# A graph attention layer: the last stage's node tiles in alternating instead of falling order of degree

## The reference

```python
qkv = x @ qkv_w + qkv_b                       # q: 32, k: 32, v: 64 columns
qe = q[s] * scale + (edge_attr @ q_rpe_w + q_rpe_b)
ke = k[t] + (edge_attr @ k_rpe_w + k_rpe_b)
ve = v[t] + (edge_attr @ v_rpe_w + v_rpe_b)
compat = einsum('ehd,ehd->eh', qe, ke)
attn = softmax of compat over the edges of node s
out = segment_sum(ve * attn, s)
return layernorm(x + out)
```

## Time and profile before

| | us |
|---|---|
| median of 3 runs | 5642.24 (5641.77 to 5651.28) |
| profiled execution | 5704.77 |
| its span | 5703.1 |
| busy: TensorE, VectorE | 4020.2, 4190.8 |
| busy: ScalarE, GpSimd | 2869.4, 3574.7 |
| the last stage in the span | about 5107 to 5703 |

### The profile page before, as it was taken

The page is one execution under the profiler, slowest core; times in us unless marked ns, Lnnn a source line. Parts: engine busy times, 40 slices in busy tenths (PEclk is TensorE's granted clock), DMA queues, the critical chain, the costliest instruction groups (busy, mean ns, idle before and its releaser), DMA issues. The chain is left out here.

```text
span 5703.1 us, 94294 instructions
## 1 busy us (share of the span) xinstructions
PE 4020.2 (70%) x18783; PEld 3567.5 (63%) x18783; DVE 4190.8 (73%) x18085; ACT 2869.4 (50%) x6600; POOL 3574.7 (63%) x3772
## 2 busy tenths in 40 slices
PE   7776776676667676776676666767766776649886
PEld 6666666666666666666666666666666666637765
DVE  7777777777777777777777777777777777759997
ACT  3554555555445554554554455545555555424555
POOL 2566666666666666666666666666666666647887
PEclk6555555555555555555555555555555555559998
DMA  6333333333333333333333333333333333379996
GB/s 184 105 109 108 106 108 106 106 110 108 104 104 108 107 105 109 106 109 104 106 112 104 106 106 106 109 106 108 108 106 108 107 107 108 104 175 384 367 351 234
DMA packets 379094, 759.55 MB, mean 133 GB/s; under 512 B 143060, under 2 KB 206875, under 8 KB 365883
## 3 DMA queue, kind: packets, MB, share of 16 engines
q1 hardware_dynamic: 255493, 385.24, 23.0%
q0 software_dynamic: 123520, 373.41, 18.2%
HBM read 570.54 MB, written 187.75 MB: 133 GB/s over the span
## 5 line engine op out<-in xcount | busy, mean ns | idle before, releaser
L634 POOL DMA_INDIRECT rec_dram<-recs,place_i x3223 | 3088.6, 958 | 1872.2 <-issue 1819.0
L670 DVE SCALAR_TENSOR_TENSOR matches<-ids_b,src_f,ps_const 128x128 bf16<-128x128 int16 (+3 forms) x3232 | 1647.3, 543 | 628.4 <-issue 580.4
L786 PE MATMUL ps_feat<-w_in,edge_in 51*128 51x128 f32 x6464 | 1684.2, 438 | 30.5 <-issue 30.4
L769 PE MATMUL ps_look<-free_rec,lo_hotT 128*128 128x98 f32 x6464 | 1609.4, 431 | 2.4 <-ACT lo_hotT L812 2.4
L786 PEld LDWEIGHTS ps_feat<-w_in,edge_in 51*128 51x128 f32 x6464 | 1441.4, 325 | 177.2 <-issue 177.2
L769 PEld LDWEIGHTS ps_look<-free_rec,lo_hotT 128*128 128x128 f32 x6464 | 1473.0, 333 | 2.6 <-ACT lo_hotT L812 2.6
L760 PE MATMUL ps_cnt<-hi_hot,lo_hot 128*128 128x98 bf16 x3232 | 407.2, 277 | 1458.8 <-DVE hi_hot L661 699.6
L824 ACT ACTIVATE free_rec<-ps_cnt 128x98 f32<-128x98 f32 x808 | 194.8, 241 | 2418.2 <-remote 2290.0
L760 PEld LDWEIGHTS ps_cnt<-hi_hot,lo_hot 128*128 128x128 bf16 x3232 | 238.6, 127 | 1671.2 <-issue 818.1
L679 DVE CUSTOM_DVE_ANT_0 picked<-hi_hot,ps_look 128x98 f32<-128x98 bf16 x3232 | 643.9, 249 | 79.1 <-issue 76.4
L812 ACT ACTIVATE lo_hotT<-lo_hotT,one 128x512 f32<-128x512 f32 x808 | 572.9, 709 | 0.0
(11 more groups left out here) (187 smaller groups left out, 2280.6 us busy)
## 6 DMA issues: line engine op xcount, KB each, us to landing
ids_b<-id_dram SPq DMA_DIRECT2D x808, 384.0 KB
rec_dram<-recs,place_i POOLq DMA_INDIRECT x3223
edge_in<-in_attr SPq DMA_DIRECT2D x808, 36.0 KB
w_in<-kv_dram SPq DMA_DIRECT2D x808, 12.0 KB
qx_dram<-qx SPq DMA_DIRECT2D x1, 4753.0 KB, 42.6
kv_dram<-kvt SPq DMA_DIRECT2D x14, 336.0 KB, 3.7
xt<-in_xT SPq DMA_DIRECT2D x14, 224.0 KB, 3.8
origin<-in_dst_tiles SPq DMA_DIRECT2D x1, 1616.0 KB, 7.7
```

The source lines that it names most:

```text
L634: pool.indirect_dma_start(rec_dram[:, :], bass.IndirectOffsetOnAxis(place_i[j][:, m:m + 1], 0), recs[j][:, m, 0:ROW], None).then_inc(scatt ...
L670: last = dve.scalar_tensor_tensor(matches[j % NS][:, junk:junk + before], ids_b[j][:, 1, 0:before], src_f[:, bass.ds(u * CT + m, 1)], ps_c ...
L769: last = nc.tensor.matmul(ps_look[j % NS][:, m, 0:NB], lo_hotT[j % NS][:, P * m:P * (m + 1)], free_rec[j % 2][:, :], start=True, stop=True)
L786: last = nc.tensor.matmul(ps_feat[j % 2][:, m, :], edge_in[j][0:K_ROWS, tile], w_in[j][0:K_ROWS, :], start=True, stop=True)
```

## The change

The order of the tiles' ranks in the last stage. The three of fewest slots stay first. Before, the others followed in falling order of slots. Now the places take in turn the rank with the fewest slots that is left and the rank with the most, from both ends to the middle, and the ranks 92 to 94 (28 slots each) come last.

```diff
 AHEAD = RB + 2
-RANK_OF = [NB - 1, NB - 2, NB - 3, *range(NB - 3)]
+TURNS = NB - 6
+RANK_OF = [NB - 1, NB - 2, NB - 3, *((k - 1) // 2 if k % 2 else TURNS - 1 - k // 2 for k in range(TURNS)), *range(TURNS, NB - 3)]
```

## The result

The changed kernel takes 5668.87 us (median of 6 runs, 5656.94 to 5677.33) where the kernel before takes 5646.76 us (6 runs, 5637.91 to 5656.27) on the same chip. The ratio of the runs is 1.0032, with a 95% interval of 1.0021 to 1.0043, so the change costs 18 us (12 to 24); the two medians lie 22 us apart, which is inside that interval. In the two traces the last stage, from its first record gather to the end of the span, takes 607.9 us after (it starts at 5047.3) and 595.4 us before (from 5107.7): 12.5 us more. What lies ahead of it is not touched by the change and differs between any two executions. The traced execution of the changed kernel is the fastest of its six (5656.94 us).

A forecast was written before the change was run, and what follows sets the result against it. VectorE was taken to bound most of the last stage, GpSimd its end; 0 - 0.7 + 4.0 + 1.3 + 0.4 + 1.5 + 0.3 = 6.8 us on the 5642.24 us median gave 5649 us, range 5637 to 5665.

The forecast's parts named there:

- TensorE's clock: Large tile's sum after a group's square-root stall runs at lowered clock; about five groups hit, +1.5 us, bounds 0 and 4.
- TensorE's window at full clock: TensorE's sum and logits edge behind a large tile outlast VectorE's shorter step; +4.0 us, bounds 0 and 8.
- The cover of the exponentials: VectorE's dot of a small tile is too short to cover ScalarE's exponentials of a large one; +1.3 us, bounds 0 and 3.
- The gathers: Large tiles' gathers have less slack before GpSimd needs them; +0.3 us, bounds 0 and 5.
- The start: Third gather is 29 slots instead of 67, so a 3.38 us wait goes; VectorE then waits 2.7 us; -0.7 us.
- The groups' cover: At a group's square root the covering dot is the small one, less cover early and more late; +0.4 us.
- Slots moved to the end: 73 slots move to the last 14 places: 6.5 us saved under VectorE, 6.6 us lost under GpSimd; together 0.
- No net effect: Rival: small tiles' spare window absorbs delayed large tiles and the start's gain comes in full; about 5642 us, chance 0.20.
- GpSimd's lag: Rival: GpSimd falls behind VectorE until its products delay TensorE's sums, and gathers come late; about 5660 us, chance 0.16.
- One of the signs: Signs of GpSimd falling behind: TensorE's sum waits for GpSimd's products, or the logits' maximum waits for GpSimd's L1238; no size.
- The gathers were not the bound: Rival: DMA engines pace the stage up to 5500 us and alternation evens their load; 5630 us, chance 0.07.

The follow-up runs named there:

- Keeping TensorE busy: Unread matmuls added behind sums ahead of TensorE's gaps; ratio to the kernel before 1.0013 in the changed order (1.0015 with none from place 80), 0.9997 in the old order.
- the pair with half sums: Kernel before and changed kernel, each with every second portion of TensorE's sums left out; ratios to the kernel before 0.9993 and 1.0007.
- Rising: Kernel before with tiles after the first three in rising order of slots, 28-slot tiles last; 5719.69 us, ratio 1.0012.
- heavy end: Kernel before in falling order, but its eleven tiles of 36 and 37 slots moved to places 84 to 94; 5707.75 us, ratio 1.0014.
- the turns with TensorE kept busy: Kernel before with small and large tiles alternating only at places 3 to 83, plus unread matmuls behind sums before place 80; 5701.45 us, ratio 1.0008.

## Why the prediction was off, point by point

The forecast was 5649 us, 6.8 us above 5642.24, with no measurable change as the likeliest outcome (0.63). The kernel became measurably slower, for which the prediction had 0.31. The ratio of 1.0032 on 5642.24 us is 5660 us, inside the range of 5637 to 5665 and above the forecast's own 5643 to 5658. The direction of the sum and its place were right, and so was the mechanism in the main, large sums that miss their window. The size was too small by about half of the stage's 12.5 and 15.9 us. That it came this near is in part luck: one term was far too small and another too large.

- *TensorE's clock.* This is the step that failed most: "about five groups are hit, less where it fitted before: +1.5", with 4 as the upper bound. Keeping TensorE busy gives 7.7, 8.5 and 9.2 us back in places 4 to 45 in three comparisons of traces, and 1.4 us in the order of before. On the chip that ran both orders both ways, 7.7 less 1.4 leaves 6.3 us for the term; the pair with half sums puts it at 6.9 to 9.5. By the medians less comes back, 4.3 and 6.6 us. I had the price of one hit about right but counted only the stalls of groups. The turns make a gap of their own at every pair: TensorE has the small tile's sum done in 3.4 us and then stands for 1.3 and 0.55 us, and behind such gaps, too, the clock fell (5121.50).
- *TensorE's window at full clock.* "Sum 3.4 us" was too much: at undisturbed sums the maximum waited 0.54 us (58 slots; 0.63 predicted) and 0.22 us (54; 0.46 predicted), and the sums of 50 to 45 slots fitted, unless GpSimd's products were late, where I had them 0.1 to 0.3 us short. The 67-slot tile waited 1.86 us and not 3.2. With TensorE kept busy the maximum waits 5.4 us in places 4 to 45 and 0.9 us in the order of before, and at most 3.5 us of that is GpSimd's. So the term is about 1 us where I had 4.0.
- *GpSimd's products.* The forecast had no term for them. They are worth about 3 us: 3.7 and 2.7 us of the waits in the two traces after, nothing before. Together with clock and window the maximum waits 10.0 and 10.4 us more in the two pairs of traces.
- *The cover of the exponentials*, +1.3: held, with 1.8 us measured.
- *The gathers*, +0.3: right in one trace, too small in the other. Behind the dot of place 4 they cost VectorE 0.2 and 2.2 us in places 4 to 45, and nothing before.
- *The start*, -0.7: about right. The dot of place 4 comes 4.1 us sooner, of which 2.8 us is work put off, so -1.3 us. VectorE waits 2.00 us for the 67-slot tile in it (5069.83), where the prediction had 2.7.
- *The groups' cover*, +0.4: VectorE waits 5.6 us for the roots in places 4 to 45 against 4.8 and 4.9.
- *Slots moved to the end*, 0: held. The last stretch left over 13.1 us against 13.2, and its steps are (81.0 - 74.6) / 13 = 0.49 us longer, as the 0.5 predicted.
- *The rivals.* No net effect is out: four traces of alternating orders with whole sums and nothing to keep TensorE busy all leave over 23 to 26 us early. GpSimd's lag gave the nearest number, 5660, and is a part of the cause. One of the signs that the prediction named for it, TensorE's sum waiting for GpSimd's products, is there. The other is not: TensorE did wait for the known part more often (11.4 us in 8 times, 4.3 before), but no wait for the maximum beyond the first followed. Its price was not the 6 us of waits and up to 5 for gathers, but about 3 us and up to 2. The gathers were not the bound either: the DMA share fell as the time rose.

What stays open: the maximum's 10.0 us, the cover's 1.8, the roots' 0.8 and the gathers' 0.2 make 12.8 of the 14.6 us in places 4 to 45; the rest has no single place. How the maximum's part divides between clock, window and GpSimd is known to some 2 us only, since a late sum can be both at half clock and behind late products, and the matmuls that kept TensorE busy delay it a little themselves. GpSimd's part was never tried by a run, for instance with fewer slots on GpSimd. The medians are not in all cases accounted for. Rising, heavy end and the turns with TensorE kept busy have ratios of 1.0012, 1.0014 and 1.0008 with stages of 593.7, 598.8 and 595.7 us, which is within the spread of before or 3 us above it. Some 4 to 8 us come with orders other than the falling one in the medians, and single traces, which differ by 4.5 us among themselves, can't place them. It was also only argued, not tried, that a clock fall needs the gaps of the pair: keeping TensorE busy filled those of the pairs and of the groups together.

## What to carry to other kernels

Where an engine must finish a job inside a neighbour's step, mixing sizes makes that window short for the large jobs and idle for the small ones; the spare of the one does not pay for the other. Idle time on an engine whose clock follows its activity has a price one job later: before evening out a load, look at what gap the small job leaves and add a sum at half clock for the large one behind it. An average that gets better, here the DMA share from 0.97 to 0.87, says nothing of the time when it was not the bound. And where an instruction waits for two engines, compare the ends of both: a summary that names one of them, or none, had hidden GpSimd here.

## What the runs showed of the hardware

The granted clock of TensorE fell to half in short stretches, not only behind gaps of 3.7 us but also behind pairs of gaps of 1.28 and 0.56 us, and not behind each: the sum at 5097.15 ran in 6.53 us behind 1.42 and 0.58 us, the one at 5121.58 in 7.54 us behind slightly shorter ones. Four such falls came at nearly the same places in two executions on chips that differ by 800 us in total: 75.4 and 77.0 us into the stage, 113.0 and 114.6, 184.6 and 186.2, 280.2 and 281.8. The Trainium skill, TensorE: Matmul & The Clock Gate, section "A second HAM failure mode: psum-queue depth-cycling", tells of a kernel whose TensorE idles briefly and often between groups of matmuls, with a clock that goes up and down as a result; this case's trace agrees, with gaps of 1.28 and 0.56 us ahead of a sum of 7.54 us instead of 5.88. With half of the matmuls left out the clock was low for 208 us of the stage, and the time didn't rise (ratio 0.9993).
